# Attention with half of its score blocks taken from their mirror images, an earlier adjacency mask, rows written out, and a new order of the experts' splits

## The reference

```python
def _L0_gnn_ref(x, adj, weight, bias, node_w, edge_w):
    node_att = jax.nn.softmax(x @ node_w, axis=0)
    h = x @ edge_w
    e = h @ h.T
    e = jnp.where(adj > 0, e, NEG_BIG)
    edge_att = jax.nn.softmax(e, axis=1)
    combined_att = node_att * edge_att
    support = x @ weight
    output = adj * combined_att @ support
    return output + bias
...
x = x + _L0_gnn_ref(_layernorm(x, axis=-1), adj, ...)
x = x + _L0_ffn_ref(_layernorm(x, axis=-1)[None], ...)[0]
x = x + _L1_gnn_ref(_layernorm(x, axis=-1), adj, ...)
x = x + _L1_ffn_ref(_layernorm(x, axis=-1)[None], ...)[0]
```

## Time and profile before

| | us |
|---|---|
| median of 3 runs | 1742.37 (1741.98 to 1742.53) |
| the profiled execution | 1740.6 |
| its span, first to last instruction | 1738.9 |
| TensorE busy | 1538.5 (88% of the span) |
| VectorE busy | 1030.1 (59%) |
| ScalarE busy | 621.7 (36%) |
| GpSimd busy | 822.0 (47%) |
| mean granted TensorE clock | 0.954 |

### The profile page before, as it was taken

One profiled execution on the slowest core, in us unless ns is written; L12 is line 12 of the kernel. 1 busy time (PEld: TensorE's weight loads), 2 busy tenths in 40 slices (PEclk: granted clock), 3 DMA queues, 4 the chain that ended last, 5 costly groups with the idle time before them and its releaser, 6 DMA issues. The chain is left out here.

```text
span 1738.9 us, 36504 instructions
## 1 busy us (share of the span) xinstructions
PE 1538.5 (88%) x9216; PEld 1285.1 (74%) x9216; DVE 1030.1 (59%) x3475; ACT 621.7 (36%) x1399; POOL 822.0 (47%) x1578
## 2 busy tenths in 40 slices
PE   5899999999999984999999918799939999999995
PEld 5788888888888873778887804355538889888894
DVE  5556666666666665555556544577656656666642
ACT  2323333333333331222332332111115555555563
POOL 0032433444444434566676612488855445555542
PEclk9999999999999996999999958899969999999998
DMA  5034433333333321564322366889626642222223
GB/s 189 4 131 169 141 136 136 136 136 136 136 135 134 125 67 41 137 150 87 51 48 48 51 139 146 157 166 173 128 81 151 161 78 36 36 36 36 36 36 97
DMA packets 198921, 183.39 MB, mean 105 GB/s; under 512 B 117867, under 2 KB 187369, under 8 KB 195353
## 3 DMA queue, kind: packets, MB, share of 16 engines
q1 hardware_dynamic: 165208, 123.95, 26.0%
q0 software_dynamic: 25984, 31.06, 11.1%
q10 hardware_dynamic: 7680, 27.84, 4.5%
HBM read 108.41 MB, written 55.65 MB: 94 GB/s over the span
## 5 line engine op out<-in xcount | busy, mean ns | idle before, releaser
L1080 PE MATMUL bank<-ffn_w_in_parts,ffn_x_t 128*128 128x512 f32 x1416 | 361.1, 403 | 1.7 <-DVE ffn_w_in_parts L1213 1.4
L1080 PEld LDWEIGHTS bank<-ffn_w_in_parts,ffn_x_t 128*128 128x128 f32 x1416 | 260.3, 191 | 55.5 <-DVE ffn_w_in_parts L1213 4.7
L1104 PE MATMUL bank<-ffn_w_out_parts,ffn_hidden_t 128*128 128x256 f32 x2124 | 283.1, 287 | 20.1 <-DVE ffn_hidden_t L1203 19.5
L1104 PEld LDWEIGHTS bank<-ffn_w_out_parts,ffn_hidden_t 128*128 128x128 f32 x2124 | 261.3, 191 | 25.7 <-issue 17.1
L828 PE MATMUL bank<-h_t,attn_h_tile 128*128 128x512 f32 (+1 forms) x1092 | 259.3, 387 | 4.1 <-POOL attn_h_tile L665 4.1
L874 PE MATMUL bank<-support,attn_probs_t 128*128 128x512 f32 x650 | 247.9, 414 | 1.8 <-DVE attn_probs_t L723 1.8
L828 PEld LDWEIGHTS bank<-h_t,attn_h_tile 128*128 128x128 f32 x1092 | 193.7, 189 | 42.2 <-issue 4.2
L1044 POOL DMA_INDIRECT x<-ffn_y,ffn_dst x118 | 198.8, 1685 | 52.5 <-issue 50.9
L704 ACT CAST attn_probs_t<-bank 128x512 fp32r<-128x512 f32 (+1 forms) x182 | 98.8, 557 | 331.6 <-PE bank L843 330.3
L723 DVE TENSOR_TENSOR attn_probs_t<-bank,attn_probs_t 128x512 fp32r<-128x512 f32 (+1 forms) x182 | 116.5, 652 | 154.6 <-ACT attn_probs_t L704 151.1
L1400 PE MATMUL bank<-normed_parts,nbr_adj_t 128*128 128x512 f16 x676 | 164.6, 390 | 42.4 <-DVE nbr_adj_t L1519 38.5
(11 more groups left out here) (270 smaller groups left out, 2350.3 us busy)
## 6 DMA issues: line engine op xcount, KB each, us to landing
adj_tile<-in_adj SPq DMA_DIRECT2D x25, 1663.5 KB, 7.1
mask<-attn_mask ACTq DMA_DIRECT2D x26, 832.0 KB, 3.4
w_w_in<-in_w SPq DMA_DIRECT2D x28, 256.0 KB
w_w_in<-in_w_t SPq DMA_DIRECT2D x28, 256.0 KB
w_w_out<-in_w_t SPq DMA_DIRECT2D x28, 256.0 KB
w_w_out<-in_w SPq DMA_DIRECT2D x28, 128.0 KB
x<-attn_x_out SPq DMA_DIRECT2D x26, 128.0 KB
xn<-attn_x_normed SPq DMA_DIRECT2D x26, 128.0 KB, 2.1
```

The source lines that it names most:

```text
L1080: ins = pe.matmul(bank[2 + 2 * slot + b][:, :], XT[:, slot, xp, k, :], WIP[:, wp, k, b * CH:(b + 1) * CH], start=n == 0 and k == 0, stop=n ...
L1104: ins = pe.matmul(bank[7][:, 0:D], HTT[:, hp, k, :], WOP[:, wp, k, :], start=n == 0 and k == 0, stop=n == 2 and k == KH - 1)
```

## The change

**Score blocks.** `ORDER[t]` has the chunks of row t begin at its own, t // 4, run to the last, and end with those left of it. A block right of the own chunk (`KEPT`, 84 of them) is computed as before and also copied out of PSUM by ScalarE (L758), into one of three slots, and stored by SyncE to a DRAM tensor (L647), in pieces of 128 fp32. VectorE's masking of such a chunk waits for the copy. A block left of the own chunk (`TURNED`, 72) is loaded from that tensor (L658, four slots) and turned by four transposes into PSUM (L914), in place of the six matmuls. The 26 own chunks are computed as before. A row of group g so has 6 - g blocks kept and g turned.

**The mask.** The adjacency tile has one buffer. Its load is issued one step earlier. The copy of h (now L726) stands ahead of the wait for it, and the mask pass (now L731) behind. The masks of rows 0 and 1 are made in the projection.

**Rows written out.** All 26 steps are written out on all engines.

**Experts.** VectorE takes the next hidden tile ahead of the first half of the split of the weights.

```diff
+ORDER = [list(range(t // 4, NC)) + list(range(t // 4)) for t in range(T)]
+KEPT = [(t, c) for t in range(T) for c in ORDER[t] if c > t // 4]
+TURNED = [(t, c) for t in range(T) for c in ORDER[t] if c < t // 4]
+KEEP_SLOTS, TURN_SLOTS = 3, 4
...
+                def keep_scores(t):
+                    for n, (row, c) in enumerate(KEPT):
+                        if row == t:
+                            c0, cn = CHUNKS[c]
+                            sp.wait_ge(raw_kept, n + 1)
+                            sp.dma_start(a["raw"][4 * c:4 * c + cn // P, t // 4, :, t % 4, :].rearrange("r p n -> p r n"),
+                                         KEEP[:, n % KEEP_SLOTS, 0:cn].rearrange("p (r n) -> p r n", n=P)).then_inc(raw_out[n % KEEP_SLOTS], 16)
+                def load_scores(m):
+                    t, c = TURNED[m]
+                    kept = KEPT.index((4 * c + 3, t // 4)) + 1
+                    for i in range(KEEP_SLOTS):
+                        sp.wait_ge(raw_out[i], (kept + KEEP_SLOTS - 1 - i) // KEEP_SLOTS * 16)
+                    if m >= TURN_SLOTS:
+                        sp.wait_ge(qk_done, score_count(*TURNED[m - TURN_SLOTS]))
+                    sp.dma_start(TURN[:, m % TURN_SLOTS, :], a["raw"][t, c].rearrange("p j n -> p (j n)")).then_inc(raw_in[m % TURN_SLOTS], 16)
...
                 def step(t, uses, slot, first, last):
                     if not known(t) or t >= 3:
                         gate.norm(pool, t - 3, uses - 2 + slot, 1 - slot)
                     if not first:
-                        pool.wait_ge(adj_in[slot], uses * 16 + (16 if last else 0))
                         pool.wait_ge(masked, (t - 1) * NC)
-                        pool.wait_ge(mask_out[slot], uses * 16)
                     pool.tensor_copy(HS[:, slot, :, :, :].rearrange("p a k n -> p (a k) n"),
                                      HT[:, :, :, bass.ds(t * P, P)].rearrange("p a k n -> p (a k) n").bitcast(F32)).then_inc(h_ready, 1)
-                    pool.tensor_scalar(NEG[:, slot, :], ADJ[:, slot, :], BIG, -BIG, ALU.mult, ALU.add).then_inc(mask_ready, 1)
+                    if not first:
+                        pool.wait_ge(adj_in, (t - 1) * 16 + (16 if last else 0))
+                        pool.wait_ge(mask_out[slot], uses * 16)
+                        pool.tensor_scalar(NEG[:, slot, :], ADJ[:], BIG, -BIG, ALU.mult, ALU.add).then_inc(mask_ready, 1)
...
+                def keep_scores(t, places):
+                    for k in places:
+                        c = ORDER[t][k]
+                        if (t, c) in KEPT:
+                            n, cn = KEPT.index((t, c)), CHUNKS[c][1]
+                            act.wait_ge(qk_done, score_count(t, c))
+                            if n >= KEEP_SLOTS:
+                                act.wait_ge(raw_out[n % KEEP_SLOTS], n // KEEP_SLOTS * 16)
+                            act.copy(KEEP[:, n % KEEP_SLOTS, 0:cn], bank[k % 4][:, 0:cn]).then_inc(raw_kept, 1)
...
-                    for c, (c0, cn) in enumerate(CHUNKS):
-                        if c == NC - 2 and midway:
+                    for k, c in enumerate(ORDER[t]):
+                        c0, cn = CHUNKS[c]
+                        if k == NC - 2 and midway:
                             midway()
-                        dve.wait_ge(qk_done, t * NC + c + 1)
+                        if (t, c) in KEPT:
+                            dve.wait_ge(raw_kept, KEPT.index((t, c)) + 1)
+                        dve.wait_ge(qk_done, score_count(t, c))
...
+                        if (t, c) in TURNED:
+                            m = TURNED.index((t, c))
+                            pe.wait_ge(raw_in[m % TURN_SLOTS], (m // TURN_SLOTS + 1) * 16)
+                            for j in range(4):
+                                ins = pe.transpose(bank[k % 4][:, j * P:(j + 1) * P], TURN[:, m % TURN_SLOTS, j * P:(j + 1) * P], ID[:])
+                        else:
+                            parts = [(0, 0), (0, 1), (1, 0)]
...
                     hidden_rest(t, uses, slot)
-                    if nxt := ahead(t, uses, slot, 2):
-                        split_w_in(nxt[0], 2, 0)
                     if nxt := ahead(t, uses, slot, 1):
                         hidden(*nxt)
                     if nxt := ahead(t, uses, slot, 2):
+                        split_w_in(nxt[0], 2, 0)
                         x_rest(*nxt)
                         split_w_in(nxt[0], 2, 1)
```

128 lines of the change are left out of this document (80 added, 48 removed).

## The result

| | before | after |
|---|---|---|
| median, 4 runs each, us | 1742.17 (1741.22 to 1742.53) | 1762.0 (1759.23 to 1763.83) |
| the profiled execution, span | 1738.9 | 1757.5 |
| mean granted TensorE clock | 0.954 | 0.941 |
| TensorE busy, us | 1538.5 | 1502.1 |

The ratio is 1.0108, with a 95% interval of 1.0092 to 1.0123. TensorE has less to do by 36 us, and the kernel is slower by 20. The forecast was 1801: slower was right, the size was not.

What follows compares the result with a forecast made beforehand. TensorE was taken to bound attention, VectorE's chain next. Stall 17.4, clock 39.7, L874's waits -1.8, projection 0 and experts +3 gave +58.3 us on 1740.6, so 1798.9, or 1801 with the median 1.8 higher; range 1718 to 1822.

Steps and rivals of the forecast that it cites:

- the stall of the rank: In attention, the early mask pass holds VectorE's L315 (router's rank); the second phase starts 0.85 or 0.58 us later, +17.4 us.
- the fall of the clock: TensorE's wait before attention's second phase lowers its clock, 2.48 us a row: 14 rows full, 4 half, +39.7 us.
- the DVE chain: VectorE's rank, masking chunks and L723 that L874, the second phase's first multiply, needs; next to bound attention after TensorE.
- E: End of L879 in an attention row, where the first phase begins; unhindered, L874 could start near E + 8.6.
- my 39: Attention's turned score blocks: at most 39 us saved, capped at 2.0 us per row by VectorE's masking.
- Stores and loads: Transfers of kept and turned blocks in attention: store assumed to land in 3.4 us, so no wait; taken as 0.
- rival D: Stall, clock fall, and stores landing as late as 7.1 us in groups 0 to 2: up to 1830 us; chance 0.04.
- The projection and the start: First two masks move into the projection, holding it by one or two stalls: 0, bounds -3 and +6 us.
- The experts: Hidden tile before weight split: 3.5 us slower in the first expert stage, 0.5 off in the second, +3 in all.
- rival A: Attention's rank stall is there but TensorE's clock holds: 1761 us, 1755 to 1780; chance 0.18.
- Rival B: No stall, the mask pass coming after the rank or not holding it; clock may fall late: 1719 to 1729; chance 0.15.
- Rival C: No stall in attention and the clock holding: 1704 us, up to 1709 with late copies; chance 0.10.

## Why the prediction was right or wrong

**The step that failed.** The mechanism was right: the stall of the rank, the later second phase, the wait, the fall of the clock. The largest error is in how many rows I charged with it. I had put VectorE's arrival at the rank at its place in the trace before, in every row, and so charged the stall at 23 steps and the clock in full at the last 14 of them. The runs showed an arrival that comes 1.0 to 1.2 us sooner from group 4 on, a stall in 17 steps, and a fall behind it in 13. The last six rows gained 12.9 us where I had charged 16.7 to five of them and taken 1.8 off for L874: 28 us of the 34 by which attention's rows were off. The price of one fall, 2.48 us where 1.5 was measured, is 7 more.

**What bounds the kernel, and the next one due: right up to group 3.** With the stall gone the DVE chain sets the first phase where I had put it: E + 8.8 in group 2 and E + 8.67 in group 3, against my E + 8.6. In group 4 it is E + 7.82 and in group 5 E + 7.7 to 8.3. There I was wrong to hold the chain "at 409.58 as now": it begins behind TensorE's first three chunks, and what is saved in these, by the narrow chunk and by turned blocks, brings it forward as well. So 2.0 us a row is not the cap: the rows of group 4 save 2.6. The 25 rows together save 38.9 us in that kernel, with the row of 27.5 us among them; that this is my 39 is chance.

**The early mask pass: right as a mechanism, wrong in the count.** L335 took 2.6 to 3.0 us in 17 rows and ended with the pass. The second phase began at E + 11.3 in the rows of groups 0 and 1, against my E + 11.4, and TensorE waited 0.8, 1.7, 2.4, 3.1 and 4.1 us in groups 0 to 4, against 0.85, 1.8, 2.5, 3.4 and 4.7. The period of the first such rows is 22.8 us, as forecast, and the pass alone in the kernel before added 14.6 us to the rows and 18.8 to the total, against my 17.4. Of the 23 steps charged, 17 had the stall. In one the pass waited 4.41 us for the store of a mask and came late, in four the rank was over in time, and one has no pass.

**The clock: mechanism right, size off.** It fell in all 13 rows with the stall where the wait was 2.4 us and more, group 2 in full, and in none of those with 1.7; the work added in the gap showed that it is the gap that does it. But I took 2.48 us from the last row of the trace before, where the lower clock lasted some 6.5 us. Here it lasted 3 and cost 1.5 to 1.6. On these 13 rows I had charged 27.3 us (4 half ones, 9 whole) and 19.9 were measured: 7 us of the error. TensorE stood still twice in the row that I took it from, at 649.38 and again at 651.61, but that is not shown to be the reason. In the kernel with the pass behind the rank, the row with one wait of 3.74 us has the lower clock for over 6 us as well,

```profile
185.00:188.00 3.00, 2.49 (x8) 2.14 (x9) 2.30 (x11) 0.28 (x1) 2.35 (x5) 0.50 0.84 219
188.00:191.00 3.00, 3.00 (x13) 2.71 (x12) 1.02 (x4) 0.59 (x1) 0.71 (x1) 0.50 1.02 400
```

and a second phase of 14.14 us, 2.7 more than without a fall; after the same 3.74 us with the third tile loaded early it is 13.11, 1.6 more. What decides between the two sizes stays open.

**Stores and loads: "taken as 0" was wrong.** I compared one transfer with one transfer. The two places where it went wrong are crowds: in row 1 the third adjacency tile and the mask's store, in row 3 two transfers of weights. My rival D had the mechanism (a copy that waits for a slot) and put it at every row of groups 0 to 2, as a landing time; it came at two rows only, as a queue: 26.3 and not 22.8 us in row 3 of the change, and TensorE's wait of 4.34 us ahead of the first full row.

**The projection and the start: wrong, +11.4 us where I had 0, -3 to +6.** Two VectorE instructions there were held, by 2.2 us each. I had named them and taken 0 without looking at which engine is late in that stretch. In the two profiles 5.5 us stand before the first scores (91.30 against 85.84). Over all profiles it is about 4: 84.8 to 87.6 in the four kernels with the old projection, 88.9 to 91.3 in the six with the new one. The two holds, 4.4 us together, are enough for that, and TensorE's waits ahead of its second batch and inside it are 3.0 to 4.5 us longer in these six than in the others. The other 6 us are ScalarE's wait for a slot and what followed it; the third tile loaded early took 5.6 of them away.

**The experts: the first stage right, the second wrong.** I forecast +0.5 at each of seven switches of the first stage, 3.5 in all, and it was +2 to +5. In the second I wrote that the split "ends no sooner" and gave 0.5; the waits at L1091 went nearly whole, half of them came back at L1080, and 3.5 more went at L1104: -8 to -10 us. My bound had it, my value did not. Of the 13.9 us gained behind attention about 5 are the neighbour stage's, whose length, to the start of the second expert stage, varies between 241 and 257 us over these profiles with no edit in it; this stays open.

**The rivals.** The time is that of rival A, 1761, by accident: A was the stall with a clock that holds, and the clock did fall. Against my sum of +58.3 the spans differ by +18.6: 34 us less in attention's rows (55.3 forecast, 21.1 measured), 11 more ahead of them, 17 less behind (+3 forecast, -13.9 measured). Errors of both signs met at 1762. Rival B's point of decision, the pass before or after the rank's end, was the right one, and it was decided row by row, by 0.02 us and less in four rows of groups 5 and 6. Rival C, no stall and a clock that holds, at 1704, is what the kernel with the one added wait comes to: 1706.5.

## What to carry to other kernels

Work that is taken from the busiest engine is worth what the next chain leaves, so find that chain first, and look at which instruction of another engine can land on it: one wait on the right semaphore was worth 50 to 55 us here, more than the 39 that attention's rows have from the blocks turned instead of computed. Then ask for which rows the chain is where the old trace has it: a saving ahead of it moves it too. A long GpSimd pass belongs where VectorE has none of the instructions that were held here (those with two SBUF inputs, and tensor_scalars), and its place has to be fixed by a wait, not left to when its data happen to arrive. Price each transfer in the row where the DMA engines are full, and not by its median.

## What the runs showed of the hardware

- A wait of TensorE of 1.7 us between dense stretches (3 rows of the change) and of 1.5 us (4 rows with added work) left the granted clock at 1.00. At 1.96 to 1.99 us it held once and fell three times; after 2.25 us and more, before the second phase, it fell in each row of these two kernels. One fall cost 1.5 to 1.6 us in most rows, and 2.7 us once after a single wait of 3.74 us.
- GpSimd's fill of 128 x 3328 bf16, which reads nothing, takes 2.87 us, hardly less than the pass that reads and computes (2.96), and holds a tensor_scalar of VectorE for as long.
- An instruction of VectorE that starts 0.02 us ahead of the pass can be held all the same (at 466.35, L335, 2.99 us, with the pass from 466.37), where one at 585.76, L339, a copy of two elements a row, was not (0.17). Of two L335 that start 0.07 us ahead of the copy of h one was held (0.70 us, at 561.14) and one was not (0.22, at 585.01).
